# A graph network's edge stage on one core: the row of source numbers stored from VectorE's transposes instead of picked word by word

## What is computed

```python
h = relu(layernorm(x))                                  # x: 50000 x 128
# resmlp_m(v) = silu(v + silu(silu(v) @ w1[m] + b1[m]) @ w2[m] + b2[m]) @ wout[m]
xx = resmlp_0(h)
xs, xp, xd = (resmlp_m(h)[idx_j] for m in (1, 2, 3))    # 12500 edges
s = xx + segment_sum((rbf @ w_rs) * xs, idx_i)
p = segment_sum((rbf @ w_rp)[:, None, :] * pij[:, :, None] * xp[:, None, :], idx_i)   # 3 per edge
d = segment_sum((rbf @ w_rd)[:, None, :] * dij[:, :, None] * xd[:, None, :], idx_i)   # 5 per edge
pa, pb = split(p @ w_pp); da, db = split(d @ w_pd)
y = s + (pa * pb).sum(-2) + (da * db).sum(-2)
out = x + resmlp_4(y)
```

## Time and profile before

| | us |
|---|---|
| median of 3 runs | 1217.9 |
| lowest, highest | 1210.91, 1219.04 |
| the profiled execution, its own time | 1216.09 |
| its span, first to last instruction | 1214.3 |
| mean granted clock of TensorE | 0.975 |
| PE, DVE, ACT, POOL busy | 1099.7, 705.0, 733.2, 460.3 |
| DMA packets in all, of these under 512 B | 269855, 166882 |

### The profile page before, as it was taken

The page is one execution under the profiler, slowest core; times in us unless marked ns, Lnnn a source line. Parts: engine busy times, 40 slices in busy tenths (PEclk is TensorE's granted clock), DMA queues, the critical chain, the costliest instruction groups (busy, mean ns, idle before and its releaser), DMA issues.

```text
span 1214.3 us, 22950 instructions
## 1 busy us (share of the span) xinstructions
PE 1099.7 (91%) x6361; PEld 721.9 (59%) x6361; DVE 705.0 (58%) x2443; ACT 733.2 (60%) x1373; POOL 460.3 (38%) x425
## 2 busy tenths in 40 slices
PE   3677998986888939999999999999988999999998
PEld 2455665664555615666666666666754666666665
DVE  9977677684566405565655666565643444444442
ACT  3456777965777835555555555556535666566654
POOL 3055666215556632655655565565340000000000
PEclk9988999998899979999999999999999999999999
DMA  9276776944665443757666666665437999999984
GB/s 274 94 228 210 229 222 207 319 141 148 197 211 189 161 100 48 80 85 79 67 73 70 67 72 77 69 66 72 90 58 202 279 277 270 267 283 271 270 272 145
DMA packets 269855, 198.49 MB, mean 163 GB/s; under 512 B 166882, under 2 KB 191498, under 8 KB 269631
## 3 DMA queue, kind: packets, MB, share of 16 engines
q1 hardware_dynamic: 231438, 152.34, 45.0%
q0 software_dynamic: 24208, 19.29, 16.3%
q10 hardware_dynamic: 14112, 25.70, 6.0%
HBM read 101.03 MB, written 96.26 MB: 162 GB/s over the span
## 4 chain that ended last, share of the span: by engine, by line
PE 73%; DVE 14%; issue 6%; another core or an unknown queue 2%; DMA 2%; ACT 1%; SPq 1%; POOL 0%; ACTq 0%; POOLq 0%; DVEq 0%
PE quad L1095 7%; PE bank L1109 7%; PE bank L1695 6%; PE quad L1101 5%; PE bank L1705 5%; PE bank L1767 4%; DVE stat L525 4%; PE bank L1737 3%; PE bank L1768 3%; PE quad L844 3%; PE bank L861 3%; DVE picked L654 3%; PE quad L851 2%; DVE onehot L637 2%
## 5 line engine op out<-in xcount | busy, mean ns | idle before, releaser
L1349 POOL DMA_INDIRECT node_sums<-rowout,row_i x98 | 156.7, 1599 | 163.8 <-ACT rowout L1625 141.3
L1016 DVE TENSOR_TENSOR rowout<-bank,xin 128x512 f32<-128x512 f32 x98 | 67.8, 692 | 142.6 <-PE bank L1109 141.7
L470 POOL DMA_INDIRECT edges_by_src<-pay,rank_i x98 | 96.4, 983 | 106.4 <-DVE rank_i L666 52.4
L470 POOL DMA_INDIRECT edges_by_low<-pay,rank_i x98 | 97.6, 996 | 95.4 <-DVE rank_i L666 43.1
L1109 PEld LDWEIGHTS bank<-wo_sb,s 128*128 128x128 f32 x784 | 102.8, 191 | 47.8 <-issue 47.8
L861 PEld LDWEIGHTS bank<-wo_sb,s 128*128 128x128 f32 x720 | 95.9, 196 | 57.9 <-issue 57.9
L1396 DVE SCALAR_TENSOR_TENSOR h<-bank,b_sb,hT 128x512 f32<-128x512 f32 (+1 forms) x75 | 55.5, 740 | 121.2 <-PE bank L1705 105.8
L74 POOL DMA_INDIRECT yin<-node_h,er x98 | 94.8, 967 | 57.9 <-issue 28.9
L654 DVE SCALAR_TENSOR_TENSOR picked<-bank,onehot 128x256 bf16<-128x256 f32 (+1 forms) x196 | 67.5, 388 | 83.0 <-PE bank L817 34.5
L754 ACT ACTIVATE xn<-xin,nbias,rnorm 128x128 f32<-128x128 f32 x216 | 104.1, 493 | 14.2 <-DVE nbias L576 14.2
L861 PE MATMUL bank<-wo_sb,s 128*128 128x128 f32 x720 | 98.2, 280 | 8.4 <-ACT rowout L793 5.8
(11 more groups left out here) (205 smaller groups left out, 2296.1 us busy)
## 6 DMA issues: line engine op xcount, KB each, us to landing
xin<-in_x_dram SPq DMA_DIRECT2D x196, 256.0 KB
node_h<-xn SPq DMA_DIRECT2D x98, 256.0 KB
out_dram<-rowout ACTq DMA_DIRECT2D x98, 256.0 KB
node_sums<-rowout SPq DMA_DIRECT2D x90, 256.0 KB
yin<-node_sums SPq DMA_DIRECT2D x53, 256.0 KB, 3.7
yin<-node_sums SPq DMA_DIRECT2D x180, 64.0 KB, 3.2
src_in_every_row<-edge_src_row SPq DMA_DIRECT2D x24, 256.0 KB
border_sums_by_tile<-border_sums SPq DMA_DIRECT2D x24, 256.0 KB
```

The costliest lines, as they stand in the source:

```text
L470: nc.gpsimd.indirect_dma_start(out=ps.dram, out_offset=bass.IndirectOffsetOnAxis(ap=rank_i[:, t:t + 1], axis=0), in_=pay[:, t, :], in_offs ...
L1349: nc.gpsimd.indirect_dma_start(out=ysum, out_offset=bass.IndirectOffsetOnAxis(ap=row_i[:, t % 2, j:j + 1], axis=0), in_=urow[:, t % 2, j, ...
```

## The change

The picks from DRAM are gone, both the ones ahead of the loop and those in it. In their place `store_src_row(k)` waits for `features_T(k)` and stores four partitions of `eA` (0, 32, 64, 96; 128 words of 512 B each; two partitions in the last group) to the same DRAM row. `load_src_row(k)` is as before but is called in iteration k, right behind the store, where before it was called in iteration k-1. VectorE gets a wait, so that `features_T(k)` doesn't overwrite a buffer of `eA` whose row is still being stored. What is computed stays the same.

```diff
-        def pack_src_row(k):
+        def store_src_row(k):
 
 
             if k < G:
-                lo, e = k * BLOCK, tiles(k) * P
-                with nc.allow_non_contiguous_dma(reason="one word of each row"):
-                    sp.dma_start(src_row[0, lo:lo + e].rearrange("(a b) -> a b", a=16), by_src[lo:lo + e, 0:1].rearrange("(a b) w -> a (b w)", a=16),
-                                 allow_slow_non_contiguous=True).then_inc(src_packed, 16)
-
-        pack_src_row(0)
+                q, n = k % 2, tiles(k)
+                sp.wait_ge(quads_T, k + 1)
+                sp.dma_start(src_row[0, k * BLOCK:k * BLOCK + n * P].rearrange("(t e) -> t e", e=P), eA[0:n * Q:Q, q, :]).then_inc(src_packed, 16)
+
@@
         for k in range(G + 1):
             store(k - 2)
             load(k + 2)
-            if k == 0:
-                load_src_row(0)
-                pack_src_row(1)
-            load_src_row(k + 1)
-            pack_src_row(k + 2)
+            store_src_row(k)
+            load_src_row(k)
@@ features_T(k)
                 if k >= 2:
+                    dve.wait_ge(src_packed, 16 * (k - 1))
                     dve.wait_ge(seg_ps, k - 1)
                     dve.wait_ge(g_ps, k - 1)
```

## The result

| | before | after |
|---|---|---|
| median, us | 1216.54 (7 runs) | 1225.12 (7 runs) |
| lowest, highest | 1210.91, 1219.04 | 1219.53, 1228.20 |
| ratio after / before | | 1.0066, 95% interval 1.0046 to 1.0087 |
| the profiled execution | 1216.09 | 1219.53 |
| mean granted clock of TensorE | 0.975 | 0.970 |

The change makes the kernel 0.66% slower, 8 us (the medians are 8.6 apart). That is within 1%, as forecast, but the time moved the other way and lies 4 us above the top of the range (1207 to 1221).

A forecast was written before the change was run, and what follows sets the result against it. TensorE was taken to bound the kernel, its edge loop hiding all but the entry. With 2.5 us gained there and all other terms 0, 1217.9 - 2.5 = 1215.4, rounded to 1215 us; range 1207 to 1221.

The forecast's parts named there:

- the part on what is moved on SyncE: Edge loop and tail: row load moved behind its store, group 3's loads sooner; all hidden from TensorE, cost 0.
- The gain at the entry: Edge stage entry: without group 0's picks its fourth gather lands sooner; 2.5 us gained, between 0 and 4.5.
- the gap of 1.40 us: Before TensorE's start at the entry: perhaps an unseen part of the fourth gather's landing, counted only in the 4.5 us.
- The store's round trip: SyncE, each group: row load waits 2.1 us for the store; hidden by 12.6 us slack, 8.5 at the tail.
- Rival C: Edge loop: store, wait and row load come onto the path; slower, 1278 us if 2.5 us over per group; chance 0.04.
- Rival D: Edge loop: relief of the DMA engines shortens it, faster by over 1% (12 us); chance 0.04.
- VectorE's added waits: In `features_T(k)`, a wait for the store of group k-2, met long before; cost zero, 2.3 us at 0.1 us each.
- A and B: Entry sooner, 1213.4 to 1216.9 us, chance 0.60; or nothing moves, 1217 to 1218, chance 0.32; together 0.92.

The follow-up runs named there:

- paced_b: Changed kernel with GpSimd's gathers of groups 2 and 3 held, so the sixteen come as 8, 4 and 4; 1204.77 us, 0.9916 (chip A); 1140.15, 0.9947 (chip B).
- before_again_b: The kernel before, unchanged, profiled once more; 1209.14 us on chip A, and 1144.23 us on chip B (there without the _b).
- after_picks: Changed kernel's order on SyncE, but with the old picks from DRAM in place of the store; 1217.52 us, ratio 1.0031 to the kernel before.
- hold23: Changed kernel, group 2's gathers held until TensorE's first output product, group 3's until VectorE's second copy of transposed rows; 1217.57 us, ratio 1.0029 to before.
- before_load3: The kernel before, picks and all, with only group 3's six loads issued right behind group 2's; 1219.47 us, ratio 1.0031.
- hold3: Changed kernel with only group 3's gathers held until VectorE's second copy of transposed rows; 1215.70 us, ratio 1.0020 to the kernel before.

## Why the prediction was wrong, point by point

**The step that failed** stands in the part on what is moved on SyncE: "Group 3's loads even come sooner: behind 459.75 before, about 450 now, since the 9.45 us wait before them is gone. Nobody waits for them at TensorE." The first sentence is right (443.8, or 449 with the node stage's end put where it was). The second asks only who waits at TensorE, and so the sum has a term of 0 there. GpSimd waited for them, 10.96 us. With that pause and the one ahead of group 2 gone, its sixteen gathers made one run, and TensorE's results reached the other engines 10.97 us late; that term measured 11.8 us in the entry. paced_b, which puts the pauses back, has no such stall. I had worked out the event and not asked what the engine behind it would do sooner. I noted what stands behind SyncE's new waits, not what stands behind the wait that went away.

The sign was in the trace of before, in a place that I read past. The node stage of chip A is full of waits for "remote", in the kernel before as well (waits of the whole span, before):

```profile
DVE picked L654 <- remote: 27.6, 6, 6.4
ACT rowout L793 <- remote: 25.2, 12, 5.6
```

There are smaller ones in the edge loop too: VectorE's `prod` (L1459) waits so 8 times in before, 1.4 us at most, which costs TensorE nothing. In the node stage GpSimd sorts the edges with indirect DMAs beside TensorE's matmuls. A profile on chip B has not one such wait in its whole span, and its node stage ends 60 us or more sooner (361.4 us against 425.0 in the two repeats of the kernel before). I took these for a bookkeeping gap of the profile. That they are the same hold as in the entry is likely, as neither is there on chip B, but not shown: no run here tested it in the node stage.

**The gain at the entry** had the right mechanism and too small a size. Forecast 2.5 us with 4.5 as the upper end; measured 4.4 in the first pair, 5.1 in the second and 4.5 on chip B. From the issue of the fourth gather to TensorE's start it took 7.15 us in before, 7.93 in before_again_b and 7.28 in before_again, and 2.7 to 2.8 us in every profile of the changed kernel. So the gap of 1.40 us, which I gave only to the upper end, belonged to the landing and went with it. The reason was right, and more than right in the loop. I had said that the gathers beside the picks suffer while the picks' own packets are cheap. The DMA queues of the steady 387 us say the same (packets, MB, share of 16 engines; q0 is GpSimd's, q1 SyncE's): first before (483 to 870), then after (485 to 872), then after_picks (479 to 866), which differs from after by the picks alone:

```profile
q0 software_dynamic: 15064, 11.05, 40.4%
q1 hardware_dynamic: 55657, 17.36, 22.4%
```

```profile
q0 software_dynamic: 15296, 11.15, 21.9%
q1 hardware_dynamic: 45264, 17.70, 19.9%
```

```profile
q0 software_dynamic: 15006, 11.02, 47.2%
```

SyncE's queue lost only 2.5 points with the picks; the packets of GpSimd's indirect DMAs, about as many and as large as before, take about half the time. It is so on chip B as well, 43.4% and 22.8%. What after_picks adds is that at the entry it is enough to issue the picks later.

**The store's round trip** went as told. Group 3 and the tail, SyncE in order of time and VectorE's masks, after:

```profile
508.41 0.50 SPq L1302 DMA_DIRECT2D edge_src_row<-eA  x1
509.99 0.34 SPq L1278 DMA_DIRECT2D src_in_every_row<-edge_src_row  x1
...
875.54 0.50 SPq L1302 DMA_DIRECT2D edge_src_row<-eA  x1
877.07 0.32 SPq L1278 DMA_DIRECT2D src_in_every_row<-edge_src_row  x1
```

```profile
526.98 0.68 DVE L1420 TENSOR_TENSOR same<-src_in_every_row,er 128x512 f32<-128x512 f32 x1
...
890.29 0.43 DVE L1420 TENSOR_TENSOR same<-src_in_every_row,er 128x256 f32<-128x256 f32 x1 [2.33 <-PE bank L1802]
```

Store to row load 1.58 and 1.53 us, where I took 2.5; the row of group 3 is issued 17 us ahead of its mask, that of group 24 13 us, and the last mask is still released by TensorE. Rival C, slower by this round trip, had the sign of the result but not its cause. The Trainium skill's rule on transfers under 512 B (DMA: Bandwidth & Descriptors, Specifications), which I had weighed, fits as far as writes to DRAM go: 512 single words took until 8.96 us after their issue in after_picks, four rows of 512 B 1.82 us for the same group in the changed kernel. Size alone is not what costs, for `nxt` of group 0, as many single words into SBUF, took 2.06 us. The Trainium skill's rule on the number of engines that a transfer uses (DMA: Bandwidth & Descriptors, Why a DMA increments its semaphore by 16 and not by 1) showed no price: 1.5 us with four packets.

**Rival D**, gain by a relief of the DMA engines, is empty as told. Windows of the changed kernel (length, busy us by engine, clock, DMA share, GB/s), first the steady part:

```profile
485.00:872.00 387.00, 386.77 (x2710) 254.65 (x2703) 237.49 (x569) 220.13 (x416) 220.56 (x170) 1.00 0.42 76
```

The share went from 0.63 to 0.42 at the same bytes, nearly all of it by the faster packets of GpSimd's queue (above), and TensorE's busy time did not move by 0.3 us. VectorE's added waits cost nothing, as said.

**The range** held what I could price and left out what I had not named. An entry of 11.8 us more is 2.6 times the whole upper end of my gain. The 0.92 that I gave to A and B rested on two cases that shared one assumption, that nothing of the entry but the gather's landing would move.

## What to carry to other kernels

When a DMA comes sooner, ask of every engine, not of the bound one alone, which instruction it lets go and what that engine then does in one piece; here GpSimd lost two pauses and issued sixteen indirect gathers in a row. Gathers that are needed one group at a time can be released one group at a time by a wait on the consumer's progress, as paced does with two waits: it gained on the one chip and cost nothing on the other. Words picked one by one from DRAM to DRAM cost little themselves and slow the indirect DMAs beside them. And a wait that the profile can't attribute, in a program on one core, is a finding to follow up before a prediction, and comparisons are made on the same chip: the change adds 0.3 to 0.7% on one and takes away 0.55% on the other.

## What the runs showed of the hardware that I had not expected

- On chip A TensorE's signals to ScalarE and VectorE come late beside and shortly after runs of GpSimd's indirect DMAs. The longest wait was 6.95 us with eight in a row in hold23 (in before_load3, also with eight, several of 1 to 2.5 us behind TensorE's recorded ends), 5.21 and 5.20 us with twelve, 9.99 and 10.97 us with sixteen, 11.12 us with twenty. Four in a row held nothing in before, before_again_b and paced_b, and 3.14 us once in hold3. So the number in a row orders the waits only roughly. On chip B nothing was held, with up to twenty in a row.
- Picking words from DRAM to DRAM beside GpSimd's indirect DMAs about doubled the time of the latter's packets, at the same bytes: 40.4 and 47.2% of the DMA engines with the picks, 21.9% without.
- The stall cost clock as well. Windows of the changed kernel in the entry:

```profile
447.00:454.00 7.00, 1.98 (x5) 0.68 (x4) 0.00 (x0) 0.00 (x0) 5.48 (x6) 0.99 0.32 66
454.00:464.00 10.00, 4.74 (x6) 1.93 (x7) 2.68 (x11) 3.55 (x7) 0.10 (x1) 0.50 0.02 7
```

  TensorE had come to 2.4 GHz, stood idle from about 449, and was granted 1.2 GHz from 454 to 464, so that the first matmuls after the stall ran at the lower level: two of L1691 took 2.04 us at 459.26 and 1.13 at 468.56.
- The stall is not explained by how busy the DMA engines are. From 447 to 457 us their share was 0.25 with 53 GB/s; in the steady part it was 0.42 with 76 GB/s, without such a stall.

**What stays open.** What in the chip couples the two engines, and why on chip A and not on chip B (there were only these two). What starts a hold within a run: in the changed kernel nine gathers had gone out before it, in hold3 once fewer than four. Whether TensorE's signals are late or its matmuls: their ends are modelled in the profile, so the trace can't tell. How many gathers in a row are safe: four held nothing most times but not always, and nothing between four and eight was run. And a rest of chance: in most profiles, of before and after alike, the start of the final stage ran at 1.2 GHz for some microseconds.
